# Retention layer of a fused decoder: the turning of the next tiles moves to another PSUM bank, and four engines' step orders are changed around it

## What is computed

```python
def _L1_attn_ref(x, q_w, q_b, k_w, k_b, v_w, v_b, g_w, g_b, o_w, o_b):
    q, k, v, g = x @ q_w + q_b, (x @ k_w + k_b) * SCALING, x @ v_w + v_b, x @ g_w + g_b
    qr, kr = _theta_shift(q, sin, cos), _theta_shift(k, sin, cos)
    qk = einsum('bhmd,bhnd->bhmn', qr, kr) * mask          # causal, decaying
    qk = qk / clip(abs(qk.sum(-1, keepdims=True)), 1.0, None)
    out = einsum('bhmn,bhnd->bhmd', qk, vr)
    out = (out - out.mean(-1)) / sqrt(out.var(-1) + 1e-05)
    return (silu(g) * out) @ o_w + o_b
...
x = x + _L1_attn_ref(_layernorm(x, axis=-1), ...)          # the stage of the change
x = x + _L1_xattn_ref(_layernorm(x, axis=-1), ctx_768, ...)  # the stage behind it
```

## Time and profile before

| | us |
|---|---|
| median of 3 runs | 1078.04 (1075.86 to 1078.6) |
| the profiled execution | 1078.04 |
| its span, first to last instruction | 1076.3 |
| TensorE busy in the span | 931.1 (87%) |
| VectorE busy | 784.8 (73%) |
| ScalarE busy | 604.6 (56%) |
| GpSimd busy | 354.5 (33%) |
| mean granted TensorE clock | 0.953 |

### The profile page before, as it was taken

One profiled execution on the slowest core, in us unless ns is written; L12 is line 12 of the kernel. 1 busy time (PEld: TensorE's weight loads), 2 busy tenths in 40 slices (PEclk: granted clock), 3 DMA queues, 4 the chain that ended last, 5 costly groups with the idle time before them and its releaser, 6 DMA issues. The chain is left out here.

```text
span 1076.3 us, 20586 instructions
## 1 busy us (share of the span) xinstructions
PE 931.1 (87%) x8076; PEld 572.4 (53%) x8076; DVE 784.8 (73%) x1495; ACT 604.6 (56%) x1052; POOL 354.5 (33%) x319
## 2 busy tenths in 40 slices
PE   2678798899588799999789998997699998999997
PEld 1333333333246555556356666675489984455554
DVE  8957966795778889877689999997487774435322
ACT  4789877899576555552154444453478872433310
POOL 1304754462337100000266667776143220000000
PEclk9969988999779899999899999999899999999999
DMA  5000000000320020000400000000200000000001
GB/s 141 0 2 1 2 1 1 2 1 1 92 85 21 1 99 1 2 2 1 159 2 2 2 2 1 3 2 2 69 1 2 2 2 1 1 1 20 21 1 40
DMA packets 16936, 21.20 MB, mean 20 GB/s; under 512 B 4596, under 2 KB 14276, under 8 KB 16456
## 3 DMA queue, kind: packets, MB, share of 16 engines
q1 hardware_dynamic: 14728, 17.79, 5.1%
q10 hardware_dynamic: 2112, 2.10, 0.6%
HBM read 17.78 MB, written 2.10 MB: 18 GB/s over the span
## 5 line engine op out<-in xcount | busy, mean ns | idle before, releaser
L625 PE MATMUL t_sc<-t_qk 32*128 32x512 f32 (+3 forms) x768 | 120.3, 584 | 41.8 <-ACT t_pT L515 16.2
L515 ACT ACTIVATE t_pT<-t_sc 128x1536 f32<-128x1536 f32 x96 | 136.7, 1452 | 29.3 <-PE t_sc L625 28.5
L3079 DVE SCALAR_TENSOR_TENSOR f_h<-f_psh,f_h 128x512 f16<-128x512 f32 x64 | 43.9, 691 | 100.6 <-ACT f_h L3105 100.5
L3135 PE MATMUL f_psh<-f_h,fs_w 128*128 128x512 f16 x512 | 114.4, 379 | 1.5 <-DVE f_h L3079 1.5
L229 POOL TENSOR_SCALAR_AFFINE_SELECT t_pT<-t_pT 128x512 f32<-128x512 f32 x64 | 72.3, 1151 | 121.5 <-ACT t_pT L515 120.9
L625 PEld LDWEIGHTS t_sc<-t_qk 32*128 32x128 f32 x768 | 54.4, 208 | 107.5 <-ACT t_pT L515 62.2
L2589 POOL TENSOR_SCALAR_AFFINE_SELECT r_att<-r_att 128x1024 f16<-128x1024 f16 x64 | 76.9, 1224 | 72.2 <-DVE r_att L2630 72.2
L3105 ACT ACTIVATE f_h<-f_psh 128x512 f16<-128x512 f32 x64 | 38.2, 597 | 108.3 <-PE f_psh L3135 108.3
L645 PE MATMUL t_ot<-t_pT,t_v 128*17 128x512 f32 (+3 forms) x768 | 75.6, 522 | 9.7 <-issue 9.1
L3135 PEld LDWEIGHTS f_psh<-f_h,fs_w 128*128 128x128 f16 x512 | 49.8, 98 | 59.0 <-issue 2.0
L1896 PE MATMUL c_pso<-ck_VO,c_pT 128*128 128x256 f16 x480 | 55.0, 273 | 1.4 <-DVE c_pT L1747 1.4
(11 more groups left out here) (514 smaller groups left out, 2229.4 us busy)
## 6 DMA issues: line engine op xcount, KB each, us to landing
x<-in_x ACTq DMA_DIRECT2D x4, 512.0 KB, 8.1
out_x<-x SPq DMA_DIRECT2D x4, 512.0 KB, 2.9
r_rcos<-in_ret_cos SPq DMA_DIRECT2D x1, 1280.0 KB, 8.2
r_rsin<-in_ret_sin SPq DMA_DIRECT2D x1, 1280.0 KB, 10.6
gw_raw<-in_gateT SPq DMA_DIRECT2D x1, 1024.0 KB, 7.4
gw_raw<-in_upT SPq DMA_DIRECT2D x1, 1024.0 KB, 9.7
gw_raw<-in_downT SPq DMA_DIRECT2D x1, 1024.0 KB, 4.8
fs_k<-in_L_ffn_k SPq DMA_DIRECT2D x1, 1024.0 KB, 7.7
```

The source lines that it names most:

```text
L515: a.activation(pT[:, at:at + 3, :].rearrange("p a s -> p (a s)"), sc[n % 2][:], ACT.Exp, scale=CURVE * CURVE / math.sqrt(2 * DH)).then_inc ...
L625: last = t.matmul(sc[n % 2][:, 512 * k + at:512 * k + at + w], qk[r, g % 2, 1, P * i:P * i + P], qk[r, g % 2, 0, q0:q0 + w], start=(part = ...
L3079: v.scalar_tensor_tensor(dst[:, 1], psh[:, i % BANKS, :], 0.0, dst[:, 0], ALU.max, ALU.subtract).then_inc(lo_done, 1)
L3135: last = mm(psh[:, i % BANKS, :], l, r, start=(k == 0), stop=(k == len(todo) - 1))
```

## The change

1. `turn_x`, `x_high` and `x_low` use bank `ptr` in place of `psq`. `turn_x(s+4)` now stands behind `gates(s-1)` in PE's step and waits, in place of `rot_read`, for `z_split` (that `z_low(s-2)` of the same step has read `ptr`) and for `k_copied`. ScalarE's `x_high(s+4)` stands behind `silu(s-1)`. DVE's `x_low` moves to the next step, behind `low(s, 0)`, as `x_low(s+3)`; `turn_qk` waits for it before it writes `ptr`, and `qk` waits for one tile less.
2. On POOL, `power(s-1)` stands between `mask(s, 0)` and `mask(s, 1)`.
3. The ten single `bn_stats` of steps 3 to 12 become four in step 11 and six in step 14, each followed by `spread`; `opening.power` goes to steps 12 and 15, `offsets` to steps 13 and 16.

```diff
             for s in STEPS:
                 mask(s, 0)
+                power(s - 1)
                 mask(s, 1)
-                power(s - 1)
                 expand(s)
-                if s in (8, 14):
-                    opening.power(g, (s - 8) // 6)
+                if s in (12, 15):
+                    opening.power(g, (s - 12) // 3)
...
             def x_low(t):
                 if inside(t) and t >= FIRST:
-                    ahead.low(v, t, psq)
+                    ahead.low(v, t, ptr)
...
             for s in STEPS:
                 low(s, 0)
+                x_low(s + 3)
                 x_center(s + 5)
...
                 values_low(s + 1)
-                x_low(s + 4)
-                if 0 <= s - 3 < opening.SPANS[1][1]:
-                    v.wait_ge(x_added, s - 2)
-                    opening.statistic(v, own, s - 3)
-                if s in (7, 13):
-                    opening.spread(v, own, (s - 7) // 6)
-                if s in (9, 15):
-                    opening.offsets(v, (s - 9) // 6)
+                if s in (11, 14):
+                    n = (s - 11) // 3
+                    v.wait_ge(x_added, opening.SPANS[n][1])
+                    opening.statistics(v, own, n)
+                    opening.spread(v, own, n)
+                if s in (13, 16):
+                    opening.offsets(v, (s - 13) // 3)
...
             def x_high(t):
-                    ahead.high(a, t, psq)
+                    ahead.high(a, t, ptr)
...
                 z_high(s - 2)
+                silu(s - 1)
                 x_high(s + 4)
-                silu(s - 1)
...
             def qk(t):
-                    upto(t_, ahead.ready, t + (2 if t + 1 >= FIRST else 1))
+                    t_.wait_ge(ahead.ready, t + 1)
...
             def turn_qk(t, n, done):
                     if n == 0:
                         t_.wait_ge(s_c, 4)
                         t_.wait_ge(rot_done, t + 1)
+                        upto(t_, ahead.ready, t + 3)
                         upto(t_, z_split, t - 3)
...
             def turn_x(t):
                 if inside(t) and t >= FIRST:
-                    t_.wait_ge(rot_read, t - 1)
-                    ahead.turn(t_, t, psq)
+                    wait(t_, z_split, t - 5)
+                    upto(t_, k_copied, t - 2)
+                    ahead.turn(t_, t, ptr)
...
                 turn_z(s - 2)
+                gates(s - 1)
                 turn_x(s + 4)
-                gates(s - 1)
```

More of the change, by code:

```diff
@@ L819, in power @@
         g.tensor_tensor(sm[:, 3, t], sm[:, 2, t], sm[:, 5, t], ALU.pow).then_inc(self.rs_ready, 1)
-    def statistic(self, v, own, t):
-        own.mark(v.bn_stats(self.st[:, t, :], self.x[:, t, :]))
     def statistics(self, v, own, n):
         for t in range(*self.SPANS[n]):
-            self.statistic(v, own, t)
+            own.mark(v.bn_stats(self.st[:, t, :], self.x[:, t, :]))
     def spread(self, v, own, n):
```

## The result

| | before | after |
|---|---|---|
| median, us | 1076.95 (1074.78 to 1078.6, 4 runs) | 1093.47 (1091.38 to 1097.08, 4 runs) |
| ratio | | 1.0155, 95% interval 1.0133 to 1.0179 |
| profiled execution, span | 1076.3 | 1089.4 |
| mean granted TensorE clock | 0.953 | 0.945 |

The change made the kernel slower by 1.55%, 16.5 us between the medians. In the changed kernel the lines of the retention stage are numbered three lower than before: 2627 is `low`, 2386 `x_center`, 2405 `x_low`, 2651 and 2653 the gate, 2672 the end of `centre`, 2692 the sum of `rotate`, 2705 the state's product, 2716 `z_low`, 2394 `turn_x`, 2605 `power`, 2586 `mask`, 2857 the projections.

The account below looks back on a forecast made before the run. The prediction took loop (a) as the floor, 13.57 us a step. Steps 2 to 11 +12.1, step 1 +0.3, steps 12 and 13 +0.2, the end +2.1: +14.7 on 1078.04, 1092.7 us; range 1083 to 1099.

Parts of the forecast that it names:

- The new loop: low, VectorE's list to z_low, turn_x, score, ScalarE's high, next low: the next low comes 2.69 us after z_low.
- loop (a): TensorE's gates to values, ScalarE's second read of them, gates again: the floor, 13.57 us; turn_x adds at least 0.32.
- loops (b) and (c): (b) VectorE's line 2689, turn_x, gates, score, ScalarE, low; (c) VectorE's own list: both fit into 13.57 us.
- The period: Time from low(s, 0) to the next: 14.98 us forecast, 1.41 above 13.57.
- The race for the port: VectorE's line 2708 comes 0.19 us behind the second mask pair's start, loses and waits; z_low ends at 12.29.
- rival 1: Line 2708 starts ahead of the mask and wins: period 14.25, +8.1, 1086 us; chance 0.21.
- Rival 2: GpSimd's pow holds the port for its length, line 2695 waits 0.45 us: 1097; chance 0.12 together with x_center caught.
- Rivals 3 and 4: Something other than z_low releases turn_x: either only loop (a) lengthens, 1083 us, chance 0.08, or Rival 4.
- Rival 4: Not slower: the rot_read wait (0.42 us a step) paces the stage; without it about 1075 us; chance 0.09.
- Steps 12 and 14, and the end: Steps 12 and 13 +0.2 for weigh held by the later mask, step 14 0, the end +2.1.
- +0.3 of step 1: Step 1 has turn_x behind gates without a z_low: +0.3 us.
- +2.1 at the end: power(14) now ahead of the mask that weigh(15) waits for: mask 3.26 us after centre in place of 1.20.

Follow-up runs that it names:

- z_low_first: The changed kernel with z_low(s-2) right behind rotate(s+2) on VectorE, ahead of state(s) and add(s-3): 1080.87 us, ratio 1.0067.
- turn_first: The changed kernel with turn_x(s+4) ahead of gates(s-1) and x_high ahead of silu again, still in ptr and waiting for z_low: 1129.28 us.
- v32_first: The kernel before with ScalarE copying the values to float32 from PSUM first, then the float16 copy from that one in SBUF: ratio 1.0001.
- center_first: The changed kernel with x_center(s+5) ahead of x_low(s+3) on VectorE: 1093.43 us, ratio 1.0172.
- state_first: The changed kernel with state(s) ahead of rotate(s+2) on VectorE: 1091.09 us, ratio 1.0154.
- gates_first: The kernel before with only gates(s-1) ahead of turn_x(s+4) and silu ahead of x_high; psq and the rot_read wait stay: 1073.94 us against 1074.07.
- stats_only: The kernel before with only the statistics in two batches (steps 11 and 14) in place of ten singles: ratio 1.0013.

## Why the prediction was right, and where its terms were off

**The loops: right.** The new loop through `z_low`, `turn_x`, `score` and `high` sets the pace. z_low_first takes it apart and turn_first lengthens it, and the time follows both (in turn_first by more than forecast, for the clock). The prediction counts seven groups on TensorE between `gates` and `values`; there are eight, and no number hangs on it. The bare length of `turn_x` in loop (a) was 0.22 us, not 0.32. That loop (a) was "the floor" overstated it: v32_first lowered it by half a microsecond and the steps fell by 0.06, to what loops (b) and (c) allow.

**The period: 15.25 for 14.98.** 0.22 of the 0.27 is the term that the prediction costed at nothing, `x_low` ahead of the gate, with an upper bound of 0.4 for just this case: `x_center` under a mask. The row it relied on the earlier trace rows showed 398 to 407 ns sixteen times, but in the steps of the kernel before, `x_center` always started ahead of the mask (627.13 against 627.29 in step 7); the row didn't show the case in question. Now it starts 0.17 us behind it. center_first confirms the 0.22. The other 0.05 is `turn_x` to `score`, 0.37 against 0.32. The Trainium skill, page "SBUF — State Buffer", section "Who interferes with whom", lists `tensor_scalar`, `x_center`'s operation, among those that can take both of VectorE's ports and then contend with GpSimd, if their operands meet certain conditions; the trace agrees that it contends, 1.06 us under a mask against 0.40.

**The race for the port: right, by 0.19 us.** The mask pair started at 639.12 and the product at 639.31, the very margin forecast, since the 0.22 us of `x_center` delayed both alike. So rival 1 lost. state_first puts its price at 0.74 us a step (15.25 to 14.51).

**The `pow` and the port: right.** Rival 2 is out: line 2692 began at 638.38, 0.46 us before the `pow` of 635.95 to 638.84 ended, and took its 0.69 us; in state_first the product ran its 0.30 us in the middle of a `pow`. The page that the prediction cites says "for the whole instruction" of VectorE's two-port modes; carried over to two SBUF inputs, as the prediction did, it doesn't hold for the `pow`, and the measurement decides.

**Rivals 3 and 4: out.** `turn_x` is released by `z_low`. The wait for `rot_read` didn't pace the stage alone: gates_first removed it and the time stayed. Rival 4 had a point in steps 8 and 9, where that wait was 1.46 and 1.74 us long in place of 0.42.

**Steps 12 and 14, and the end: too small, +5.1 for +2.3.** (The +0.3 of step 1, which lies ahead of these, didn't come either: 12.18 us against 12.27.) Step 12 lost 1.0 us to TensorE's clock, which the sum has no term for. In the timeline of TensorE the same group takes 0.49 us at 702.40 and 0.79 us at 703.79, and the projection behind it 1.91 for 1.47:

```profile
702.40 0.49 PE L2845 MATMUL r_pso<-r_u,r_qkT 128*128 128x132 f32 x2
...
703.79 0.79 PE L2845 MATMUL r_pso<-r_u,r_qkT 128*128 128x132 f32 x2
...
705.73 1.91 PE L2857 MATMUL r_psq<-ra_w,ra_xT 128*128 128x512 f16 x6
```

From the first half of `score(12)` to the second TensorE takes 6.47 us where it took 5.17, and from there to `gates` 6.79 us as before. It isn't a fixed price of the change: in center_first, with the same statistics in step 11, the clock stayed at 1.00 and step 12 took 13.27 us. Step 14 lost 1.8 us: the six `bn_stats` and a spread that met a mask (one of its small sums took 1.01 us) delayed `low(15, 0)`, and what was to take that up didn't; stats_only shows the same step at 14.42 by itself. Of the "+2.1 at the end" the mask's start is right: 3.32 us behind `low(15, 1)`, where it was 1.28 before (741.59 to 742.87), +2.04.

```profile
752.36 1.22 DVE L2627 TENSOR_TENSOR r_att<-r_pss,r_att 128x1024 f16<-128x1024 f32 x1
...
755.68 2.58 POOL L2586 TENSOR_SCALAR_AFFINE_SELECT r_att<-r_att 128x1024 f16<-128x1024 f16 x2
...
758.32 0.81 PE L2845 MATMUL r_pso<-r_u,r_qkT 128*128 128x132 f32 x2 [5.97 <-POOL r_att L2586]
```

The wait for POOL grew from 4.55 us to 5.97, just short of the "over 6" forecast; behind it TensorE starts at half clock (0.81 us for 0.49).

**The total agrees better than its parts, and that is luck.** 1092.7 was forecast and 1093.47 measured, but the stage grew by 19.5 us, not 14.4. The forecast started from 1078.04, at the upper end of what the kernel before takes: its later medians are 1073.15 to 1074.07 (1070.47 to 1079.8 in single executions). All 37 executions of the changed kernel that were timed have a median of 1093.59, 19.5 to 20.4 us above these, though perhaps on other chips. So a base some 4 us too high covered terms some 5 us too small. What lies behind the stage hardly varies (313.7 to 315.5 us), so what varies is ahead of it; why it does stays open.

## What to carry to other kernels

When a transfer buffer is shared, look at what is queued behind the waiting instruction: `turn_x` needed 0.4 us and could wait, but the next `score` stood behind it, and so `z_low`, a late item of VectorE's list, was drawn into the loop that sets the pace. Before moving work off a wait, check whether the engine would wait at that place without it too, as TensorE did in loop (a). And an instruction that gains by leaving a busy port may only hand the collision to the next one.

## What wasn't expected of the hardware

- TensorE's granted clock fell in four stretches of the changed kernel to 0.89 or 0.90, where it had been 1.00 throughout from 557 to 732 us before.

```profile
598.00:613.00 15.00, 14.22 (x169) 10.01 (x168) 12.64 (x24) 6.37 (x12) 8.97 (x7) 0.90 0.01 2
628.00:644.00 16.00, 15.26 (x194) 11.03 (x191) 12.65 (x24) 7.34 (x12) 8.08 (x7) 0.89 0.00 1
673.00:688.00 15.00, 14.20 (x168) 10.07 (x165) 12.64 (x24) 6.38 (x12) 8.97 (x7) 0.90 0.01 1
703.00:718.00 15.00, 14.26 (x175) 10.06 (x172) 13.05 (x29) 6.48 (x11) 9.73 (x8) 0.89 0.00 1
```

  Before these, TensorE had waited 0.74 us ahead of `gates` and then 1.23, 1.24, 2.40 and 0.91 us ahead of `turn_x`. state_first, which waits only 0.28 us ahead of `turn_x`, kept 1.00 in the first two of these stretches. But the stretches between, with the same waits, kept 0.98 to 1.00 in the changed kernel too, so what decides it in a single step isn't shown. In plain steps it cost nothing: the period is 15.24 to 15.26 us in slow stretches and in others. In step 12 it cost 1.0 us, and in turn_first it has a part in the 1.75 us by which the ten steps came out longer than forecast (18.60 each for 16.85).
- The `pow` on 128x16 takes 2.89 us without holding VectorE's two-input instructions, and the 0.44 us by which it was longer before go with what runs at its start. The fourteen profiles hold 224 executions of it. In 110 a VectorE sum of two SBUF tensors (`rotate`'s, or `values_low`) was running when it began, and these take 3.33 to 3.36 us; the other 114 take 2.89 to 2.93.
